# Gated cross-attention with a feed-forward product on one core: two of the four pair sums of each query half merged by an accumulating transfer, and half of the query stacks loaded a quad sooner

## What is computed

```
q, k, v = Wq @ layernorm(x) + bq,  Wk @ ctx + bk,  Wv @ ctx + bv      # 16 heads of 32 channels
dot  = mask * (q^T k) / sqrt(32) - (1 - mask) * 1e6                   # per head 1024 queries x 1024 keys
out  = v @ (softmax(dot over the keys) * mask)^T
x    = x + tanh(g_xattn) * out
x    = x + tanh(g_ffn) * ffn(layernorm(x))                            # operands rounded to fp8, product 512 x 1024 x 1024
```

## Time and profile before

| | |
|---|---|
| timed runs | 2498.09, 2505.27 and 2502.59 us, median 2502.59 |
| the profiled execution's own time | 2498.55 us |
| its span, first to last instruction | 2496.9 us |
| granted TensorE clock, mean | 0.996 of full speed |
| busy | PE 98%, DVE 79%, POOL 66%, ACT 56% of the span |
| DMA engines, mean busy share in attention | about 0.4 |

### The profile page before, as it was taken

How to read it: one execution, slowest core, us unless ns; L and a number is a source line. 1 busy time by engine, 2 the same in 40 slices (tenths; PEclk the granted TensorE clock), 3 DMA queues, 4 the chain that set the end, 5 groups by cost and what they waited for, 6 DMA issues and landing times.

```text
span 2496.9 us, 40504 instructions
## 1 busy us (share of the span) xinstructions
PE 2441.7 (98%) x13116; PEld 1382.0 (55%) x13177; DVE 1960.7 (79%) x3259; ACT 1387.1 (56%) x2606; POOL 1643.2 (66%) x1259
## 2 busy tenths in 40 slices
PE   7999999999999999999999999999999999999997
PEld 5888888875444444444444444444444444444442
DVE  6677776687788888888888888888888888888885
ACT  3333333315666666666666666666666666666664
POOL 2443333426777777777777777777777777777775
PEclk9999999999999999999999999999999999999999
DMA  6766666664444444444444444444444444444411
GB/s 245 262 243 237 234 235 235 227 188 100 94 102 98 102 101 102 97 94 95 94 93 100 92 92 92 92 92 101 92 93 95 99 101 102 98 101 97 104 45 56
DMA packets 241807, 313.48 MB, mean 126 GB/s; under 512 B 75000, under 2 KB 142648, under 8 KB 241624
## 3 DMA queue, kind: packets, MB, share of 16 engines
q1 hardware_dynamic: 230776, 275.56, 44.0%
q10 hardware_dynamic: 10848, 35.66, 4.0%
HBM read 199.83 MB, written 101.38 MB: 121 GB/s over the span
## 4 chain that ended last, share of the span: by engine, by line
PE 94%; DVE 1%; DMA 1%; issue 1%; POOL 1%; ACT 1%; SPq 0%; POOLq 0%; ACTq 0%; DVEq 0%
PE bank L863 22%; PE bank L893 20%; PE bank L848 20%; PE bank L878 19%; PE bank L904 9%; PE bank L940 4%; PE bank L933 1%; POOL pair_sum L398 1%; DMA q_st<-qx_scr 0%; DMA w_nat<-in_L_xattn_Wk_dram 0%; DMA v_scr<-stage 0%; ACT probs L715 0%; DVE x_raw L1043 0%; PE bank L802 0%; PE bank L924 0%
## 5 line engine op out<-in xcount | busy, mean ns | idle before, releaser
L398 POOL TENSOR_TENSOR pair_sum<-probs 128x512 f32<-128x512 f32 x1020 | 1279.2, 1286 | 399.0 <-ACT probs L715 399.0
L1143 DVE TENSOR_REDUCE part_max<-bank 128x1 f32<-128x512 f32 x2048 | 1276.6, 682 | 242.7 <-PE bank L878 229.2
L715 ACT ACTIVATE probs<-bank 128x512 f32<-128x512 f32 x2048 | 1067.4, 604 | 601.7 <-PE bank L863 578.7
L863 PE MATMUL bank<-q_st,k_st 100*128 100x512 f32 x2048 | 866.3, 425 | 6.0 <-ACT probs L715 6.0
L878 PE MATMUL bank<-k_st,q_st 98*128 98x512 f32 x2048 | 817.4, 399 | 8.3 <-DVE part_max L1143 6.5
L863 PEld LDWEIGHTS bank<-q_st,k_st 100*128 100x128 f32 x2048 | 387.4, 190 | 410.3 <-issue 211.2
L893 PE MATMUL bank<-probs,v_t 128*32 128x512 f32 x4096 | 545.6, 605 | 0.0
L878 PEld LDWEIGHTS bank<-k_st,q_st 98*128 98x128 f32 x2048 | 388.7, 190 | 129.2 <-DVE part_max L1143 15.8
L389 POOL TENSOR_TENSOR stage_lo<-stage,stage_hi 128x512 fp32r<-128x512 f32 x128 | 186.6, 1483 | 137.7 <-ACT stage_hi L661 136.2
L904 PE MATMUL bank<-pair_sum,ones 128*32 128x512 f32 x2040 | 265.5, 592 | 0.0
L661 ACT ACTIVATE stage_hi<-stage 128x512 fp32r<-128x512 f32 x128 | 80.2, 633 | 205.1 <-DVE stage L1007 142.9
(11 more groups left out here) (112 smaller groups left out, 2007.3 us busy)
## 6 DMA issues: line engine op xcount, KB each, us to landing
k_st<-k_scr SPq DMA_DIRECT2D x96, 512.0 KB
q_st<-q_scr SPq DMA_DIRECT2D x192, 256.0 KB
c_raw<-in_ctx_dram ACTq DMA_DIRECT2D x32, 512.0 KB, 7.0
k_scr<-stage_hi SPq DMA_DIRECT2D x64, 256.0 KB, 2.5
k_scr<-stage_lo SPq DMA_DIRECT2D x64, 256.0 KB, 2.7
v_scr<-stage SPq DMA_DIRECT2D x64, 256.0 KB, 2.9
q_scr<-stage_hi SPq DMA_DIRECT2D x64, 256.0 KB, 2.4
q_scr<-stage_lo SPq DMA_DIRECT2D x64, 256.0 KB, 2.7
```

Of the source, the lines that this page charges most:

```text
L398: nc.gpsimd.tensor_tensor(pair_sum[:, r % 2, h], probs[:, a, h], probs[:, a + 1, h], ALU.add).then_inc(pair_done, 1)
L715: nc.scalar.activation(probs[:, c % PR, h, :], s_bank_of(n, k)[:, :], ACT.Exp).then_inc(exp_done, 1)
L863: nc.tensor.matmul(s_bank_of(n, k)[:, :], k_st[p][0:KS, h, j * P:(j + 1) * P], q_st[p][0:KS, th, h, :], start=True, stop=True).then_inc(sc ...
L1143: nc.vector.tensor_reduce(part_max[:, th, sh, at:at + 1], x_bank_of(n, "tile", k)[:, :], AX, ALU.max).then_inc(max_done, 2)
```

## The change

Two of the four pair sums of each half are no longer summed by PE one by one. The sums now lie in four buffers (`sums`): the two of `pair_sum`, and `stage` and `stage_hi`, free by then. After pair 1, and after pair 5, POOL issues a transfer that adds the buffer of pair 0 (4) into that of pair 1 (5), 128 x 2048 elements of fp32, 1 MB (`merge`). PE takes three groups a half in place of four: in slots 35 (pair 2), 39 (pairs 0 and 1, merged) and 43 (pair 3), and in slots 3 (pair 6), 7 (pairs 4 and 5) and 11 (pair 7) of the next period. Before the first pair of the first quad POOL waits until all stores of the first stage have landed (`wait_stage_free`). On SP, `stack_q` is called once a half: half 0 of quad n + 2 behind `load_v` of period n, half 1 of quad n + 1 at the start of period n as before. The diff, cut to its core:

```diff
-        stacked = [sem(f"stacked{i}") for i in range(TH)]
+        k_stacked = sem("k_stacked")
+        q_stacked = [sem(f"q_stacked{i}") for i in range(TH)]
...
+        merged = [sem(f"merged{i}") for i in range(TH)]
...
+            sums = [pair_sum[:, 0], pair_sum[:, 1], stage[:, :, :], stage_hi[:, :, :].bitcast(F32)]
...
-            STACK_DMAS = (8, 4)
+            STACK_DMAS = 4
...
+            DEN_AT = {35: 0, 39: 1, 43: 2}
+            DEN_AFTER = {3: 3, 7: 4, 11: 5}
+            NG = 6
+            SUM_OF_GROUP = (2, 1, 3, 6, 5, 7)
+            GROUP_OF_SUM = {1: 1, 2: 0, 3: 2, 5: 4, 6: 3, 7: 5}
+            MERGED = (0, 4)
...
+                    def wait_stage_free():
+
+                        for i in range(STG):
+                            pool.wait_ge(v_stored[i], 16 * B * (GV // STG))
+                            pool.wait_ge(qk_stored[i], 32 * B * (2 * GK // STG))
+
+                    def wait_sum_free(n, r):
+
+                        m, was = (n, r - 4) if r >= 4 else (n - 1, r + 4)
+                        if m < 0:
+                            return
+                        if was in MERGED:
+                            pool.wait_ge(merged[was // 4], 16 * (m + 1))
+                        else:
+                            pool.wait_ge(den_done, NG * m + GROUP_OF_SUM[was] + 1)
+
                     def add_pair(n, r):
                         a = 2 * r % PR
-                        if counted(SJ * n + r - 1):
-                            pool.wait_ge(den_done, SJ * n + r - 1)
+                        wait_sum_free(n, r)
                         for h in range(QH):
...
-                            nc.gpsimd.tensor_tensor(pair_sum[:, r % 2, h], probs[:, a, h], probs[:, a + 1, h],
+                            nc.gpsimd.tensor_tensor(sums[r % 4][:, h], probs[:, a, h], probs[:, a + 1, h],
                                                     ALU.add).then_inc(pair_done, 1)
+
+                    def merge(n, th):
+
+                        pool.wait_ge(pair_done, QH * (SJ * n + 4 * th + 2))
+                        pool.dma_start(sums[1], sums[0], accum_op=ALU.add).then_inc(merged[th], 16)
...
                     def period(n, p):
                         for r in range(SJ):
+                            if n == 0 and r == 0:
+                                wait_stage_free()
                             if real(n) and (n, r) != (LAST, SJ - 1):
                                 add_pair(n, r)
+                            if real(n) and r % 4 == 1:
+                                merge(n, r // 4)
...
                     def stack_k(m, p):
-                        if m % QUADS == 0:
-                            wait_stored(m // QUADS)
                         if m == 0:
+                            wait_stored(0)
                             sp.wait_ge(stored, 16 * 5)
...
-                    def stack_q(m, p):
+                    def stack_q(m, th, p):
+                        if m > 0 and m % QUADS == 0 and th == 0:
+                            wait_stored(m // QUADS)
+                        if m >= 2:
+
+                            sp.wait_ge(scores_ready, NSLOT * (m - 2) + 32 * (th + 1))
+                            sp.wait_ge(x_ready, NSLOT * (m - 1))
...
                     def period(n, p):
                         if n > 0 and real(n + 1):
                             stack_k(n + 1, 1 - p)
-                            stack_q(n + 1, 1 - p)
+                            stack_q(n + 1, 1, 1 - p)
...
                         if real(n + 1):
                             load_v(n + 1, 1 - p)
+                        if real(n) and real(n + 2):
+                            stack_q(n + 2, 0, p)
                         if real(n):
                             move_den(n, 0)
...
                     def copy_den(m, th):
-                        act.wait_ge(den_done, SJ * m + 4 * (th + 1))
+                        act.wait_ge(den_done, NG * m + 3 * (th + 1))
...
+                        if i == 0:
+                            pe.wait_ge(k_stacked, 16 * STACK_DMAS * (m + 1))
                         if i % 32 == 0:
-                            pe.wait_ge(stacked[th], 16 * STACK_DMAS[th] * (m + 1))
+                            pe.wait_ge(q_stacked[th], 16 * STACK_DMAS * (m + 1))
...
-                    def denominators(m, r):
-                        th, i = r // 4, r % 4
+                    def denominators(m, g):
+                        th, i = g // 3, g % 3
+                        r = SUM_OF_GROUP[g]
...
-                        pe.wait_ge(pair_done, QH * SJ * m + QH * (r + 1))
+                        if i == 1:
+                            pe.wait_ge(merged[th], 16 * (m + 1))
+                        else:
+                            pe.wait_ge(pair_done, QH * SJ * m + QH * (r + 1))
                         for h in range(QH):
-                            last = nc.tensor.matmul(d_bank[D * h:D * (h + 1), :], ones[:, :], pair_sum[:, r % 2, h, :],
-                                                    start=(i == 0), stop=(i == 3))
+                            last = nc.tensor.matmul(d_bank[D * h:D * (h + 1), :], ones[:, :], sums[r % 4][:, h, :],
+                                                    start=(i == 0), stop=(i == 2))
...
-                        if k % 8 == 3:
-                            if k >= 19 and real(n):
-                                denominators(n, (k - 19) // 8)
-                            if k < 19 and real(n - 1):
-                                if n - 1 == LAST and k == 11:
-                                    denominators_last()
-                                else:
-                                    denominators(n - 1, 6 + k // 8)
+                        if k in DEN_AT and real(n):
+                            denominators(n, DEN_AT[k])
+                        if k in DEN_AFTER and real(n - 1):
+                            if (n - 1, DEN_AFTER[k]) == (LAST, NG - 1):
+                                denominators_last()
+                            else:
+                                denominators(n - 1, DEN_AFTER[k])
```

21 lines of the change are left out of this document (11 added, 10 removed).

## The result

The changed kernel takes 2568.02 us (median of 4 runs, 2564.09 to 2570.38), the kernel before 2503.93: a ratio of 1.0257, 95% interval [1.024, 1.0275]. It is **slower by 64 us**; 25 were predicted. The profiled execution took 2567.88 us with a span of 2566.1, 69.2 more than before.

A forecast was written before the change was run, and what follows sets the result against it. PE was taken to bound the kernel, with DVE having 18% to spare. Start +10.6, rest of quad 0 -1.7, quad 1 -1.0, last quad 0, ordinary quads +17.1: +25.0 on 2498.55, so 2524 us; range 2502 to 2565.

The forecast's parts named there:

- Of the merge only its landing counts ... hidden, cost nil: Slots 7 and 39: the transfer lands in 10.3 us, before its group some 17 to 20 us later; cost nil.
- POOL's issue: POOL issuing the transfer before pairs 2 and 6: taken as 1.28 us, with no row showing one.
- slot 27, with L1218's wait: Ordinary quad: the removed group gains 0.86 us, DVE's wait for POOL's additions stalls the max tile by 0.7.
- slots 51, 55: Ordinary quad: removing slot 51's group gains 0.64 us, since ACT's normalisation stalls slot 55's scores by 0.22.
- slots 59, 63, with L90's wait: Ordinary quad: DVE's L90 and L93 limit slot 63's max tile; L90 waits 0.2 us for POOL; net -0.14.
- The groups stand where DVE and ACT need the time: Ordinary quad: four removed groups gain only 2.03 us, two new ones cost 1.72; 0.31 us gained at best.
- Phase of DVE and POOL: Slots 27 and 59: DVE waits for POOL's additions through their shared lock; 0.9 us a quad, nil to about 1.6.
- two full waits of 1.25: Upper bound on DVE's waits for POOL's additions in a quad: about 1.6 us after subtracting the slack.
- The start: Quad 0: pair 0 waits for the last stores until 589.5 us, delaying slot 19; +10.6 us once.
- (4): Behind slot 19: POOL's issue holds the lock, DVE's negation is late by 1.28 us; 2561 us or more; chance 0.13.
- (3): Merge lands late, at 21.1 us: slot 7 waits 5.4 us, slot 39 waits 1; 2722 us; chance 0.10.
- The signs: Expected in the trace: max tiles of slots 23 and 63 waiting 0.7 and 0.5 us, first pair at about 589.5.

The follow-up runs named there:

- run 2: The changed kernel with each accumulating transfer cut from 8192 to 32 bytes of each partition, POOL's issue kept: 2539.32 us, ratio 1.0144.
- run 1: The changed kernel without the accumulating transfer, the merged group taking pair 1 (or 5) alone: 2525.46 us, ratio 1.0101.

## Why the prediction was wrong

**The failed step** is "Of the merge only its landing counts ... hidden, cost nil". The landing was indeed hidden: 7.4 us against medians of 19 and 17 us from the issue to the group, no wait of PE's groups for it. But a transfer is also a load on a shared resource. I had read that the engines are "mostly idle" and had asked who is late *for* it, never who is late *behind* it. With POOL's issue kept and the bytes gone (run 2) the kernel takes 28.7 us less (33 by the spans), nearly all of it in the ordinary quads: (61.12 - 60.16) x 29 = 27.9. That is the price of the hold. A second term was put at nil without a reason: what POOL's issue does to DVE in quads 0 and 1, 10.4 us (run 1 against the changed kernel). Accumulate against copy, 2568.02 - 2529.68 = 38.3 us, holds both: 29 in the ordinary quads, 7.6 in quads 0 and 1, the rest elsewhere. The prediction had no term for the clock either.

**The rest of the sum held, but as a sum, and that is luck.** Without the transfer the kernel takes 2525.46 us; the prediction, which costed it at nil, said 2524. The ordinary quads came out 7 us cheaper than forecast, quads 0 and 1 cost 4.6 more, and the end and the first stage the rest. Term by term (us; run 1 against the kernel before, by slots and periods of the traces):

| term | predicted | measured |
|---|---|---|
| ordinary quad, no transfer's hold | +0.59 | +0.41 as a rule, +0.34 on the mean |
| slot 19 and 23 | -0.19 | -0.03 |
| slot 27, with L1218's wait | -0.16 | -0.39 |
| slots 51, 55 | -0.64 | -0.60 |
| slots 59, 63, with L90's wait | -0.14 | -0.27 |
| slots 7 and 39 | +1.72 | +1.70 |
| 29 ordinary quads | +17.1 | +9.9 |
| slots 18 and 19 of quad 0: the start's wait less a group | +10.6 | +13.4 |
| slots 20 to 22 of quad 0, at the lower clock | none | +0.5 |
| rest of quad 0 | -1.7 | -1.7 |
| quad 1 | -1.0 | +0.3 |
| last quad and what follows | 0 | +1.7 |
| first stage | none | +3.4 |
| POOL's issue in quads 0 and 1 | none | +10.4, on top of run 1 |

- **The groups stand where DVE and ACT need the time**: right. Eight groups became six and the quad got longer. Without a transfer and with the start mended the kernel is still at 1.0024, though it sums less. Quad 1 gained nothing because slots 55 and 63 gave back what 51 and 59 had gained.
- **Phase of DVE and POOL**: right for L1218 in ordinary quads (1.06 us against 1.1), though the stall was 0.47 and not 0.7. Without any issue L1218 takes 1.06 us too, so it isn't the issue that moves it there; it comes with the groups that are gone. Wrong for quads 0 and 1, where I had let the wait end with one addition. The three waits there of 2.93, 2.93 and 3.37 us are longer than the "two full waits of 1.25" of my bound.
- **POOL's issue** takes 0.87 us, not 1.28, with 0.30 of waiting ahead of it. No row then had its price, and in the ordinary quads it had no effect.
- **The start**: the mechanism was right, the size 2.8 us short in run 1 (2.2 in the changed kernel). Pair 0 began at 591.64 against 589.5, and slot 19 at 597.29 against 595.4 for its max tile.
- **Rivals.** (4) gave nearly the measured time by a mechanism that did not occur: the negation that lies inside POOL's issue takes 0.18 us, and the two in the second half 0.17 each, as before. (3) did not occur here. In the run with the later transfer PE does wait for the merge, but at landings of 8.4 and 12.4 us and with a late `inv_b` and a lower clock besides; that its 2776 us are near my 2722 is chance.
- **The signs** that I had named nearly all came: the max tiles of slots 23 and 63 late by 0.83 and 0.59 us, the first pair at 591.64, L1218 at 1.06, a quarter of the groups gone, no wait of the groups for a transfer. None of them asked who waits for the small transfers, so they could not have shown the step that failed.

Of what I had drawn on in the Trainium skill, the box on DVE blocking DMAs in "SBUF — State Buffer" is not borne out by any run here: the issue takes 0.87 us at 1399.60, with L100 and L101 beside it, and 0.88 in the second half, without them. By the Trainium skill, "DMA: Bandwidth & Descriptors", "Anatomy of one DMA", I had estimated 4.4 us for the transfer; the plain copy measured 5.3 and the accumulating one 7.4, so that estimate is short by the addition above all.

Left open: why just quads 10, 17 and 26 take 2 to 4 us more. What they do is the same wait of ACT at slot 38, 1.3 to 1.5 us longer, in quad 10 with `inv_scr` at 6.6 us. In quads 10 and 26 the transposes are late at slot 31 before it, and 1.5 us more follow at slot 39 at the lower clock; but why the transfers are later in these quads no run shows. Not tried: smaller accumulating transfers with gaps between them, and `inv_scr` ahead of the transposes on SP with all else in place.

## What to carry to other kernels

A large transfer in the background has two costs. One is its landing; the other is that for the microseconds for which it holds the DMA engines, small transfers issued behind it come late. In a chain of two only the one that leaves while the engines are held pays: here `inv_scr`, not `inv_b`. What counts is the delay beyond the slack of whoever waits. Before you add one, list every small transfer that leaves in its shadow, who waits for it, and with what slack.

A wait of the engine that bounds the kernel can cost more than its length. Look at the granted clock of the stretch behind it: here PE ran at 0.50 behind several of the longer ones.

Where an engine is nearly full in some slots, taking work from the engine that bounds the kernel brings only what the next one has to spare in that slot; and moving its steps elsewhere changes its meeting with an engine it shares a lock with. Both are read slot by slot, not from shares of busy time.

## What was not expected of the hardware

- An accumulating transfer of 1 MB within SBUF (128 x 8192 bytes, from POOL's queue) lands after 7.4 us, a copy of the same bytes after 5.3, 32 bytes a partition after 2.0. The engines are held 13.3% of the span against 7.4% for the same packets.
- While the accumulating one moved, little of SP's queue got through: 8 KB landed after 4.1 us in place of 1.4, transposes after 7.7 in place of 3.2, 16 KB after 7.79, and 256 KB issued together with it after 10.43 in place of some 5. With the plain copy 8 KB landed after 1.8.
- Behind or during waits of PE the granted TensorE clock fell to 0.50 for a few microseconds: eight products with v took 1.94 us in place of 1.07. In the runs with many stalls the mean granted clock from 700 to 2400 us was 0.94 to 0.97.
- An operation of DVE that meets POOL's additions waits sometimes for one (1.06 us) and sometimes for all that are left in the row (2.93, 2.96, 3.37 us). "SBUF — State Buffer" in the Trainium skill says that the lock is held for a whole instruction; the trace shows it passed from one instruction to the next of the same engine.
